# First attention as one stream: projections and maxima of the next group of heads beside each unit's scores

## What is computed

```python
def reference(...):
    x = L0_attn_a_x                                  # 1 x 2048 x 128
    x = x + _L0_attn_a_ref(_layernorm(x), ...)       # the stage of this change
    x = x + _L0_ffn_ref(_layernorm(x), ...)          # six layers of windowed attention and ffn
    x = x + _L0_attn_b_ref(_layernorm(x), ...)       # 16 heads of 64
    x = x + _L0_ffn_ref(_layernorm(x), ...)
    return x

def _L0_attn_a_ref(x, w_qkv, w_out):
    qkv = jnp.einsum('bsi,oi->bso', x, w_qkv)
    q, k, v = ...                                    # 16 heads of 8
    logits = jnp.einsum('bhsd,bhtd->bhst', q, k) * scale
    logits = jnp.where(mask, logits, neg_inf)        # causal
    probs = jax.nn.softmax(logits, axis=-1)
    out = jnp.einsum('bhst,bhtd->bhsd', probs, v)
    return jnp.einsum('bsi,oi->bso', out, w_out)
```

## Time and profile before

| | |
|---|---|
| median of 3 runs | 6712.57 us (6699.28 to 6715.85) |
| the profiled execution | 6713.21 us, its span 6711.4 us |
| busy over the span | TensorE 88%, VectorE 69%, GpSimd 63%, ScalarE 50% |
| mean granted TensorE clock | 0.912 |
| the page's first six slices of 40 (about 168 us each) | TensorE 8 to 9 tenths busy, VectorE 3 to 6, GpSimd 0, clock 6 to 7 tenths |

### The profile page before, as it was taken

One profiled execution on the slowest core, in us unless ns is written; L12 is line 12 of the kernel. 1 busy time (PEld: TensorE's weight loads), 2 busy tenths in 40 slices (PEclk: granted clock), 3 DMA queues, 4 the chain that ended last, 5 costly groups with the idle time before them and its releaser, 6 DMA issues. The chain is left out here.

```text
span 6711.4 us, 186028 instructions
## 1 busy us (share of the span) xinstructions
PE 5936.8 (88%) x75443; PEld 3979.3 (59%) x75443; DVE 4646.9 (69%) x5424; ACT 3337.3 (50%) x3929; POOL 4232.0 (63%) x2048
## 2 busy tenths in 40 slices
PE   8998996888888888889999999999688888888887
PEld 4334335766666666755555555555366666666665
DVE  5335436888888888856556556554288888888886
ACT  1431344666666666622333333333366666666664
POOL 0000006888888787714666666668788888888884
PEclk6665667999999999989999999999899999999999
DMA  0000002222222222200000000000022222222221
GB/s 24 1 1 1 1 1 63 68 68 67 66 72 63 68 67 60 64 13 1 1 1 1 1 1 1 1 1 1 23 66 72 63 71 63 69 64 71 63 66 46
DMA packets 187701, 254.25 MB, mean 38 GB/s; under 512 B 60348, under 2 KB 81336, under 8 KB 186680
## 3 DMA queue, kind: packets, MB, share of 16 engines
q1 hardware_dynamic: 186840, 242.02, 13.9%
HBM read 38.98 MB, written 1.57 MB: 6 GB/s over the span
## 5 line engine op out<-in xcount | busy, mean ns | idle before, releaser
L1943 POOL TENSOR_TENSOR XB<-XB,Pb 128x1024 f32<-128x1024 f32 x448 | 1073.6, 2396 | 383.0 <-ACT Pb L1903 342.3
L909 POOL TENSOR_TENSOR sin_qk<-raw_qk,rot 128x512 f32<-128x512 f32 x768 | 1006.4, 1332 | 87.4 <-ACT raw_qk L817 56.3
L1903 ACT ACTIVATE Pb<-slot 128x1024 f32<-128x1024 f32 x512 | 505.2, 1023 | 875.5 <-PE slot L1800 821.6
L1951 DVE TENSOR_REDUCE b_pmax<-slot 128x1 f32<-128x1024 f32 x512 | 623.2, 1221 | 425.1 <-PE slot L1686 425.0
L925 POOL TENSOR_TENSOR rot_out<-rot_out,sin_qk 128x1024 f32<-128x1024 f32 x192 | 602.0, 3135 | 394.4 <-DVE rot_out L983 393.3
L942 POOL TENSOR_TENSOR inv_norm<-norm2c,minus_half 128x16 f32<-128x16 f32 x192 | 662.7, 3452 | 170.4 <-DVE norm2c L1084 169.9
L282 POOL TENSOR_TENSOR rstd<-variance,minus_half 128x4 f32<-128x4 f32 x20 | 19.8, 1008 | 1074.2 <-DVE variance L291 1074.2
L531 PE MATMUL slot<-w_hi,x_hi 128*128 128x512 f32 x1152 | 547.8, 476 | 63.9 <-POOL w_lo L900 44.6
L782 ACT ACTIVATE qT<-slot 128x1024 f32<-128x1024 f32 x192 | 197.1, 1027 | 748.2 <-PE slot L538 748.2
L938 POOL TENSOR_TENSOR inv_norm<-norm2c,minus_half 128x16 f32<-128x16 f32 x192 | 559.4, 2913 | 0.0
L1684 PE MATMUL slot<-KA,QA 128*128 128x512 f32 x1024 | 470.6, 460 | 68.3 <-DVE b_pmax L1951 56.8
(11 more groups left out here) (213 smaller groups left out, 13336.4 us busy)
## 6 DMA issues: line engine op xcount, KB each, us to landing
VW<-V SPq DMA_DIRECT2D x1152, 128.0 KB
VW<-V SPq DMA_DIRECT2D x768, 64.0 KB
w_raw<-in_Wqkv SPq DMA_DIRECT2D x36, 512.0 KB, 3.7
Wo<-in_Wo SPq DMA_DIRECT2D x12, 512.0 KB, 4.2
W<-in_W SPq DMA_DIRECT2D x12, 341.0 KB, 3.1
consts<-in_shape_constants SPq DMA_DIRECT2D x1, 2436.5 KB, 8.9
QB<-rows_dram SPq DMA_DIRECT2D x128, 2.0 KB
W<-in_W SPq DMA_DIRECT2D x24, 64.0 KB
```

Of the source, the lines that this page charges most:

```text
L909: ins = pool.tensor_tensor(dst[:, :, x, :], src[:, :, 1 - x, :], tab, ALU.mult)
L1903: act.activation(Pb[:, at % B_RING, :], slot[n % 2][:, :], ACT.Exp).then_inc(s["b_exp"], 1)
L1943: pool.tensor_tensor(b_sum[:, window % 2, :], Pb[:, (at - 1) % B_RING, :] if k == 1 else b_sum[:, window % 2, :], Pb[:, at % B_RING, :], A ...
L1951: dve.tensor_reduce(b_pmax[:, n // 2, n % 2:n % 2 + 1], o[:, :], AX.X, ALU.max).then_inc(s["b_max"], 1)
```

## The change

The loop over rounds is unrolled, and becomes one stream over all units of all four groups of heads (`A_ALL`). `QT`, `KT` and `V4` are there twice. The projections and maxima of a group are cut into 85 "pairs" (`A_PAIRS`), each of which uses the two banks of slot 2 once: `("qk", b)`, `("v",)` and 80 of `("max", i, u, hp)`: 128 queries by at most 512 keys, heads 2 hp and 2 hp + 1 in one bank each, the masks behind both mains. Only the first group's pairs run alone; those of group g + 1 are spread over the 80 half units of group g (`pairs_beside`). Scores have slots 0 and 1. The maxima are combined, turned and sent for each block of 512 queries (`dve_block_maxima`, `pe_turn`, `A_TURN`: block 0, 1 and 2 of the next group beside units 11, 17 and 29, block 3 beside unit 9 of its own group). The copies `gq_w` to `go_w` are gone. Row sums are now taken as 16 columns, inverted as 128 x 16, and spread by 16 small matmuls (`spread`), in units 1 and 2 of the next block; `project` is in unit 3.

```diff
+        A_PAIRS = [("qk", 0), ("v",)]
+        for b_ in range(NB):
+            if b_:
+                A_PAIRS.append(("qk", b_))
+            A_PAIRS += [("max", i, u, hp) for i in range(4 * b_, 4 * b_ + 4) for u in range(b_ + 1) for hp in range(2)]
+        A_TURN = {11: 0, 17: 1, 29: 2}
+        A_TURN_ALONE = {14: 0, 31: 1, 56: 2}
+        def pairs_beside(n, half):
+            at, of = 2 * n + half, 2 * len(A_UNITS)
+            return range(-(-len(A_PAIRS) * at // of), -(-len(A_PAIRS) * (at + 1) // of))
...
+        def pe_pair(pe, g, j):
+            if kind == "max":
+                if last[0] != "max":
+                    pe.wait_ge(s["a_split"], START + NB * g + i // 4 + 1)
+                width = min(512, 128 * (i + 1) - 512 * u)
+                for e in range(2):
+                    if last[0] == "max":
+                        pe.wait_ge(s["a_max"], START + tiles_before(g, j) - 1 + e)
...
+                    mm = pe.matmul(slot[2][:, 512 * e:512 * e + width], QT[par][rows, 128 * i:128 * i + 128],
+                                   KT[par][rows, 512 * u:512 * u + width], start=True, stop=True)
+                    if u < i // 4:
+                        mm.then_inc(s["a_s1"], 1)
+                if u == i // 4:
+                    for e in range(2):
+                        pe.matmul(slot[2][:, 512 * e + width - 128:512 * e + width], ident_b[:, :], mask_qk[:, :],
+                                  start=False, stop=True, skip_group_check=True).then_inc(s["a_s1"], 1)
+            else:
+                if last_g >= 0:
+                    if last[0] == "max":
+                        pe.wait_ge(s["a_max"], START + tiles_before(g, j))
+                    else:
+                        pe.wait_ge(s["a_split"], START + NB * g + 1)
...
-            with pe.Fori(0, 4) as g:
...
+            for j in range(len(A_PAIRS)):
+                if j in A_TURN_ALONE:
...
+                pe_pair(pe, 0, j)
...
+            scores(0, 0)
+            scores(0, 1)
+            for at, (g, n) in enumerate(A_ALL):
+                qb, k = A_UNITS[n]
+                last, turned = NB * g + qb - 1, turn_beside(g, n)
+                for half in range(2):
+                    if at + 1 < len(A_ALL):
+                        scores(at + 1, half)
+                    if half:
+                        values(at)
+                        if k == 1 and last >= 0:
+                            pe.wait_ge(s["a_lo"], START + turns_done(g, n))
+                            sums(last)
+                        if k == 2 and last >= 0:
+                            spread(last)
+                        if k == 3 and last >= 0:
+                            project(last)
+                        if turned is not None:
+                            pe.wait_ge(s["a_yadd"], START + max(last + 1, 0))
+                            pe.wait_ge(s["a_lo"], START + turned)
+                            pe_turn(pe, turned)
+                    if g + 1 < A_GROUPS:
+                        for j in pairs_beside(n, half):
+                            pe_pair(pe, g + 1, j)
```

More of the change, by code:

```diff
@@ new lines, in values @@
+            def values(at):
+                g, n = A_ALL[at]
+                qb, k = A_UNITS[n]
+                c0 = max(0, 128 * (k - 4 * qb))
+                if n == 0:
+                    pe.wait_ge(s["a_vsb"], START + g + 1)
+                pe.wait_ge(s["a_exp"], START + 2 * at + 2)
+                if k == 0:
+                    pe.wait_ge(s["a_osb"], START + NB * g + qb)
+                for hh in range(4):
+                    mm = pe.matmul(slot[3][32 * hh:32 * hh + 32, c0:512], V4[g % 2][:, k, hh, :],
+                                   Pa[:, (2 * at + hh // 2) % 4, 512 * (hh % 2) + c0:512 * (hh % 2) + 512],
+                                   start=(k == 0), stop=(k >= 4 * qb), skip_group_check=True)
+                mm.then_inc(s["a_pv"], 1)
@@ new lines, in sums, with spread @@
+            def sums(last):
+                pe.wait_ge(s["a_osb"], START + last + 1)
+                pe.wait_ge(s["a_yadd"], START + last)
+                heads = const("sum_rows").rearrange("p (h r) -> p h r", r=32)[:, :, 0]
+                for c in range(4):
+                    mm = pe.matmul(slot[3][:, 512 + 4 * c:516 + 4 * c], Oa[:, 128 * c:128 * c + 128], heads,
+                                   start=True, stop=True)
+                mm.then_inc(s["a_bc"], 1)
+            def spread(last):
+                pe.wait_ge(s["a_inv"], START + last + 1)
+                for c in range(4):
+                    for hh in range(4):
+                        at = 4 * c + hh
+                        mm = pe.matmul(slot[3][32 * hh:32 * hh + 32, 512 + 128 * c:640 + 128 * c],
+                                       sum_inv[:, at:at + 1].to_broadcast([128, 32]), ident, start=True, stop=True)
+                mm.then_inc(s["a_ispread"], 1)
@@ new lines, in dve_first, with invert, scale @@
+            for j in range(len(A_PAIRS)):
+                if j in A_TURN_ALONE:
+                    dve_block_maxima(dve, A_TURN_ALONE[j])
+                    dve_turn(dve, A_TURN_ALONE[j])
+                dve_pair(dve, 0, j)
+            def invert(last):
+                dve.wait_ge(s["a_bc"], START + last + 1)
+                dve.reciprocal(sum_inv[:, :], slot[3][:, 512:528]).then_inc(s["a_inv"], 1)
+            def scale(last):
+                dve.wait_ge(s["a_ispread"], START + last + 1)
+                dve.tensor_tensor(On[:, :], Oa[:, :], slot[3][:, 512:1024], ALU.mult).then_inc(s["a_on"], 1)
```

392 lines of the change are left out of this document (198 added, 194 removed).

## The result

| | before | changed |
|---|---|---|
| median | 6701.39 us (6680.14 to 6715.85) | 6767.2 us (6763.9 to 6796.54) |
| ratio | | 1.0099, 95% interval 1.008 to 1.0118 |
| the profiled execution | 6713.21 us, span 6711.4 us | 6796.54 us, span 6794.8 us |
| mean granted TensorE clock | 0.912 | 0.900 |

The change makes the kernel slower by 1%, 66 us by the medians.

A forecast was written before the change was run, and what follows sets the result against it. TensorE, busy 88% of the span, was taken as the bound. The first attention stage summed to 172 + 3 x 239 + 112 = 1001 us against 982, +19, so 6732 us; range 6635 to 6805.

The forecast's parts named there:

- Direction: Whole kernel: slower, +19 us to 6732 us; chance of slower by over 0.3% put at 0.46.
- First group alone: Stretch before the first scores: 85 pairs with nothing beside them take 172 us, against 117 before.
- Which clock?: Groups with pairs beside: clock 0.60, high a fifth of the time, so 239 us between 261 (low) and 180 (high).
- the unit and its extras: Groups with pairs, low clock: units 206 us plus 55 for projections, sums, spread, project and turns, 261 us a group.
- Rival 3: Groups with pairs: the clock hardly ever rises, values being diluted; +89 us, 6802; chance 0.23 shared with another slow rival.
- One unit with pairs: Groups with pairs beside: a full unit takes 5.35 us at 1.2 GHz, 3.6 at 2.4; diagonal units 4.85 and 3.3.
- the first projection and the values' one: Both stand in one half unit; in-order TensorE waits for both chains, adding 9.5 us per group at the low clock.
- Last group: Last scores and values, nothing beside: 112 us, from 128.2 with cheaper masks, a shorter reciprocal and the spread.
- Masks: Diagonal scores, masks behind two mains: 1.3 us saved 16 times a round, 21 us at the low clock, fewer at high.
- Transfer, exponentials, SP's queue at nothing: Attention stage: the block transfers, ScalarE's exponentials and SP's queue add no time.
- The turns: Turns of the maxima: 1.5 us each; three make 4.5 us in the first group alone, four make 6 per later group.
- What side by side hides: Maxima beside scores and values: hides VectorE and the transfer, but most TensorE work only where its instructions get shorter.

The follow-up runs named there:

- e10c_no_maxima: The changed kernel with the maxima matmuls and reduces of groups two to four left out, turns and transfers kept: 6470.5 us, 0.9647 of the kernel before.
- e2_three_slots: The changed kernel with the first group's pairs going in turn through three slots instead of slot 2 alone: 6723.68 us, 1.0012 of the kernel before.
- e3_masks_before: The kernel before with only the masks' order changed: two heads' mains issued together, then their two masks: 6615.14 us, 0.9855.
- e9c_masks_apart: The changed kernel with each main matmul of the scores followed by its own mask again: 6861.1 us, 1.0229 of the kernel before.
- e1_fill2: The changed kernel plus two unread full-array matmuls ahead of the pair in each unit with pairs beside it: 6784.36 us, 1.0101 of the kernel before.
- e5_full4: The changed kernel plus four unread 128-row matmuls behind the values in 24 of a group's 40 units with pairs beside: 6860.59 us, 1.0188 of before.
- e6_quarter4: The same kernel as e5_full4, but its four added matmuls use 32 rows of the array instead of 128: 6910.0 us, 1.0261 of the kernel before.

## Why the prediction was right or wrong

- **Direction: right.** The stream is slower, +66 us by the medians and +76 in the profiled stage against +19 forecast. Its maxima aren't hidden in the sum (e10c_no_maxima), and the first group runs alone in one slot (e2_three_slots).
- **First group alone**, 172 us forecast, 176.0 measured. Right, by its step: one slot, each bank through matmul and maximum in turn.
- **Which clock?** This is the step that failed: "I take the middle of 0.50 and 0.70, a clock of 0.60". Measured 0.54 to 0.55, the high level for 9% of the time instead of a fifth. The prediction's own formula gives 261 / (1 + 0.09 x 0.45) = 251 us for that, against its 239; measured 247.2, 259.8 and 259.3, mean 255.4. So of the 16.4 us that a group was under-sized, 12 are the clock and 4 the unit and its extras. Over three groups that is 49 us (36 of them the clock) of the 57 between the stage's forecast and its measure; 4 and 4 are the first and the last stretch. The middle was a choice without a row behind it. The row that was nearest was there: the maxima stretch, 98% busy with matmuls of 24 rows, at 0.50; from start to start, more of the new groups' time goes to mains of 24 and 26 rows (298 of 766 us) than to the values on 128 rows (185), where in scores and values before the two were alike (46 and 47 of 129). Rival 3, which decides under a mean clock of 0.55, was the nearest to what happened; it gave +89.
- **One unit with pairs**, 5.35 us forecast at 1.2 GHz. Plain full units take 5.18, or 4.76 where the pair and the scores behind it are on other quarters of the rows: the walk had them one after the other. The wait of the second pair is there as walked. That the unit and its extras came out only 4 us too small a group is in part luck, because errors cancel: diagonal units were walked at 4.85 us, and those of the second group's first block take 6.4 to 6.8, with masks on both the scores and the pair; the stretch with the first projection and the values' one takes 20.0 us from values to values (722.27 to 742.29), where a unit plus 9.5 was forecast.
- **Last group**, 112 forecast, 115.8 measured; right.
- **Masks**, 21 us a round at the low clock: in the kernel before they are worth 27 in the last round (e3_masks_before), since the clock rises with them, and in the last group of the stream 22 (e9c_masks_apart). The price of the instructions was right, what they do to the clock wasn't in it.
- **Transfer, exponentials, SP's queue at nothing: right.** No wait of TensorE for the rows stands in the stage. TensorE's matmuls do stand idle for exponentials, 13 us a group, but 12 of them are at the projections, where ScalarE's three instructions for the projection come ahead of the exponential in its queue (3.48 us at 380.32, after the projection at 373.11); that chain was priced. The turns, priced at 1.5 us each, have TensorE's matmuls waiting for 2.5 us in all in the first group, and not beside the units.
- **What side by side hides.** The prediction said that it "hides VectorE and the transfer". The transfer, yes. VectorE, not in the sum: a group's maxima cost 104 us beside the units (e10c_no_maxima) where maxima and transfer took 101.5 before. The walk had VectorE's waits in its numbers, the sentence hadn't; up to half of the 104 is the clock of the other work, which neither had.

What stays open: how high the clock would rise for a given share of the array; the two sizes expected for that (e1_fill2, e5_full4) were missed. The profiled execution of the changed kernel is 29 us over its median, and its mean clock is 0.900 where the other four have 0.904. An estimate from these: some 60 us more at the lower level, at which the work of 30 us takes 60, so the clock would account for the 29; in which stage it fell isn't known.

## What to carry to other kernels

Before laying one stage beside another, write down what each lets the other keep: here the maxima brought narrow matmuls that took the high clock from scores and values, got one slot where they had four, and tiles of 512 where they had 1024, and in the sum nothing was hidden. Look first for what can be had inside the old order; here grouping the masks behind two mains (-1.5%) and running two heads' maxima side by side (together -2.3%) beat the new order even when its two faults were repaired (-0.6%). And when a stretch's clock is to be forecast, start from the row whose matmuls look most alike in rows of the array used, not from the middle of two rows: here 0.50 was nearer to the measured 0.545 than 0.60 was.

## What the runs showed of the hardware that was not expected

- Same count of matmuls, same columns, a higher busy share, but 32 rows instead of 128: granted clock 0.53 instead of 0.65 (e6_quarter4, e5_full4).
- Moving 32 mask matmuls a round behind the second main raised the clock of scores and values from 0.70 to 0.82, though it made no matmul wider and left TensorE's busy share lower (88.5 of 101.7 us, 87%, against 117.3 of 128.9, 91%; e3_masks_before). The same values and masks then come in less time.
- Matmuls on different quarters of the rows start together also when they belong to different streams and write different slots: pair and scores at 428.82 and 428.83 in the changed kernel; on the same quarters the scores start 0.60 later (407.07 and 407.67).
